# Turning the queries a unit sooner, one semaphore per cache gather, and a projection split over two units, in a two-layer attention and mixture kernel

## What is computed

```python
# attention (query and key are normed and rotated first, k and v go into the cache)
k_all, v_all = k_blocks[block_tables], v_blocks[block_tables]      # window of 256 keys + own 64
scores = einsum('bghtd,bgsd->bghts', qg, k_all) * SCALE
p = softmax(where(allowed, scores, -inf))
o = einsum('bghts,bgsd->bghtd', p, v_all)
y = einsum('bto,do->btd', o, Wo)
# experts
logits = clip(y @ gate_w.T, -50, 50)
top_w, top_idx = top_k(logits, 2); rw = softmax(top_w)
deltas = softmax(expert_atom_weights) @ atoms
weighted = deltas * sigmoid(importance)                            # sparse change of W per expert
out = y @ W.T + segment_sum(y[:, cols] * (rw . weighted[top_idx]), rows)
x = x + out
```

## Time and profile before

| | |
|---|---|
| median of 3 runs | 985.54 us (982.99 to 990.58) |
| the profiled execution | 991.06 us, its span 989.5 us |
| busy: TensorE matmul, VectorE, ScalarE, GpSimd | 90%, 66%, 39%, 44% |
| chain of work that ended last | PE 50%, DVE 16%, DMA 14%, issue 8% |
| stages | layer 0 to 455, attention to 807, lists to 827, expert tiles to 989.5 |
| granted clock of TensorE, mean | 0.94 to 455; 0.73 in 455 to 500; 0.87 in 500 to 525; 0.92 to 1.00 in each pair from 525 to 782 |

### The profile page before, as it was taken

One profiled execution on the slowest core, in us unless ns is written; L12 is line 12 of the kernel. 1 busy time (PEld: TensorE's weight loads), 2 busy tenths in 40 slices (PEclk: granted clock), 3 DMA queues, 4 the chain that ended last, 5 costly groups with the idle time before them and its releaser, 6 DMA issues.

```text
span 989.5 us, 15012 instructions
## 1 busy us (share of the span) xinstructions
PE 888.9 (90%) x4085; PEld 637.7 (64%) x4085; DVE 651.2 (66%) x1875; ACT 382.9 (39%) x869; POOL 431.0 (44%) x492
## 2 busy tenths in 40 slices
PE   5699998999899999967898999998999985999994
PEld 5688656874687478525566666665656654888773
DVE  5654589867886799495657767777766762444332
ACT  2522232224222332464545556766655530111110
POOL 3302334444344300005434665556565523666773
PEclk8599998999999999995879999999999996999998
DMA  8645454023302310544223344434333204743772
GB/s 230 239 127 197 159 198 138 1 49 81 92 1 46 120 43 1 173 147 118 77 60 93 76 115 104 113 104 128 102 97 90 61 23 130 223 148 87 126 114 31
DMA packets 66360, 105.44 MB, mean 107 GB/s; under 512 B 29811, under 2 KB 31107, under 8 KB 66158
## 3 DMA queue, kind: packets, MB, share of 16 engines
q0 software_dynamic: 30368, 50.69, 20.2%
q1 hardware_dynamic: 34974, 52.14, 17.0%
q10 hardware_dynamic: 944, 1.74, 0.6%
HBM read 91.63 MB, written 37.49 MB: 130 GB/s over the span
## 4 chain that ended last, share of the span: by engine, by line
PE 50%; DVE 16%; DMA 14%; issue 8%; POOL 4%; ACT 4%; SPq 2%; DVEq 0%; POOLq 0%; ACTq 0%
PE bank L799 14%; PE bank L810 8%; PE bank L948 6%; PE bank L933 6%; DMA mine<-list_dram 6%; PE bank L922 4%; PE bank L913 3%; PE bank L832 3%; DMA q_t<-q_dram 3%; POOL out_dram L2044 2%; DMA up_raw<-in_up_t 2%; DMA out_dram<-z_sb,mine 2%; PE bank L892 2%; PE bank L942 2%; DVE raw L1612 2%
## 5 line engine op out<-in xcount | busy, mean ns | idle before, releaser
L549 POOL DMA_INDIRECT kv_t<-kv_dram,own_new x64 | 68.9, 1076 | 179.3 <-DMA kv_dram<-kv_out 111.6
L933 PE MATMUL bank<-pT,kv_t 128*128 128x256 f32 (+1 forms) x384 | 115.6, 422 | 0.0
L832 PE MATMUL bank<-wqkv,x1T 128*128 128x512 f32 x256 | 112.1, 593 | 1.4 <-ACT x1T L1098 1.4
L1680 DVE CUSTOM_DVE_ANT_0 prob<-bank,mask 128x320 f32<-128x320 f32 x128 | 57.8, 487 | 71.8 <-PE bank L913 65.4
L1187 ACT ACTIVATE pT<-bank 128x384 f32<-128x384 f32 x128 | 55.8, 486 | 118.9 <-PE bank L922 118.3
L534 POOL DMA_INDIRECT kv_t<-in_kv_cache,own_cache x64 | 67.0, 1047 | 57.8 <-PE bank L933 39.3
L1086 ACT ACTIVATE silu<-bank,gs 128x512 f32<-128x512 f32 x44 | 30.2, 690 | 158.2 <-PE bank L799 158.2
L832 PEld LDWEIGHTS bank<-wqkv,x1T 128*128 128x128 f32 x256 | 47.7, 190 | 57.5 <-issue 57.5
L933 PEld LDWEIGHTS bank<-pT,kv_t 128*128 128x128 f32 (+1 forms) x384 | 64.1, 193 | 30.1 <-issue 22.2
L799 PE MATMUL bank<-hT_hi,gate_w 128*128 128x512 f32 x176 | 72.7, 413 | 6.9 <-DVE hdn L1523 5.3
L1256 ACT ACTIVATE zT_hi<-bank 128x512 fp32r<-128x512 f32 x44 | 26.3, 598 | 131.9 <-PE bank L1024 131.9
(11 more groups left out here) (313 smaller groups left out, 2005.2 us busy)
## 6 DMA issues: line engine op xcount, KB each, us to landing
table_dram<-wexp POOLq DMA_DIRECT2D x16, 512.0 KB, 2.9
xr<-in_x SPq DMA_DIRECT2D x4, 1024.0 KB, 6.8
yx_dram<-x SPq DMA_DIRECT2D x16, 256.0 KB, 2.3
q_dram<-q_out SPq DMA_DIRECT2D x16, 256.0 KB, 2.1
kv_dram<-kv_out SPq DMA_DIRECT2D x16, 256.0 KB, 2.3
early_stage<-table_dram SPq DMA_DIRECT2D x8, 512.0 KB, 8.1
q_t<-q_dram SPq DMA_DIRECT2D x16, 256.0 KB, 3.6
stage<-table_dram SPq DMA_DIRECT2D x16, 256.0 KB, 3.2
```

What stands on the lines that cost most here:

```text
L549: pool.indirect_dma_start(kv_t[q % KVB][0:rows, c, :], None, kv_dram, bass.IndirectOffsetOnAxis(own_new[0:rows, at:at + 1], 0), bounds_che ...
L832: mm = pe.matmul(bk(2 * (j % 2) + half), x1T[:, k, j * P:(j + 1) * P], wqkv[:, k, half * T:(half + 1) * T], start=(k == 0), stop=(k == KT ...
L933: mm = pe.matmul(bk(O_BANKS[q % 2])[:, gp * 2 * P:(gp + 1) * 2 * P], kv_t[q % KVB][0:rows, c, v:v + 2 * HD], pT[0:rows, n % 2, c, :, :].re ...
L1680: dve.tensor_tensor_reduce(prob[s % PROBS][:, :], bk(s % 2)[:, 0:KEYS], mask[:, s // 4 % 2, :], MASKED, MASKED, ALU.add, ALU.min, mx[:, s ...
```

## The change

1. SyncE issues `load_q(p + 2)` and `store_y(p - 2)` (instead of `store_y(p - 1)`) after the pair's first `load_piece`.
2. TensorE turns the next pair's queries at the end of the unit with at 0, after `values`, instead of in the unit with at 1. ScalarE's `qT_copy` now waits for the last score that reads the old `qT_hi`, VectorE's stands before the two `normalize`. `y_copy(p - 2)` stands in ScalarE's unit with at 0, after `kT_copy`, instead of `y_copy(p - 1)` at 3.
3. `project_o` is made in two halves of two k-steps, one at the end of the unit with at 2, one at the end of that with at 3. `y_ps` is given after the second.
4. The cache gathers of chunk 0 and of chunk 1 have a semaphore each (`cache_in`), and each gather of new rows waits for the cache gather of its chunk alone. `round_entry` goes; VectorE converts the entry's row number (one step more in `place_entry`).
5. The tail: `project_o(14)` comes after `logits(15)`, `project_o(15)` after `places(15)`; the last pair's `oT` has a buffer of its own; the sums of the counts are made inside `places(15)`; the steps to the row numbers are fewer and stand first (`rows_ready`), those to the experts' numbers come after; loading `mine` waits for the first list's entries alone, and for the second's from tile 22 on. Constants for this are made before the loop.

```diff
@@ gather_cache, gather_new
-                                        bounds_check=POOL_ROWS - 1, oob_is_err=False).then_inc(kv_gathered[q % KVB], 16)
+                                        bounds_check=POOL_ROWS - 1, oob_is_err=False).then_inc(cache_in[c], 16)
...
                 at = q * NCH + c
+                pool.wait_ge(cache_in[c], 16 * max(q + 1, 2))
+                pool.sem_inc(taken, 1)
                 pool.indirect_dma_start(kv_t[q % KVB][0:rows, c, :], None, kv_dram,
@@ SyncE
-                    if p >= 1:
-                        store_y(p - 1)
-                    if p + 2 < PAIRS:
-                        sp.wait_ge(qT_ps, p + 2)
-                        load_q(p + 2)
+                        if at == 0 and p >= 2:
+                            store_y(p - 2)
+                        if at == 0 and p + 2 < PAIRS:
+                            sp.wait_ge(qT_ps, p + 2)
+                            load_q(p + 2)
+                store_y(PAIRS - 2)
                 store_y(PAIRS - 1)
 
-                sp.wait_ge(entry_stored, 32 * PAIRS)
-                sp.wait_ge(tiles_ready, 1)
+                sp.wait_ge(rows_ready, 1)
+                sp.wait_ge(entry_stored[0], 16 * PAIRS)
                 for i in range(ALL_TILES):
+                    if i == TILES:
+                        sp.wait_ge(entry_stored[1], 16 * PAIRS)
@@ TensorE
+                    if p == PAIRS - 1:
+                        for n, part in enumerate((ab, counts)):
+                            mm = pe.matmul(bk(5)[:, 4 * E:6 * E], ones_sq[:, :], part[:, :, :].rearrange("p a e -> p (a e)"),
+                                           start=(n == 0), stop=(n == 1))
...
                     if n + 2 < UNITS:
                         score(n + 2)
-                    if at == 1 and p + 1 < PAIRS:
-                        if p >= 2:
-                            pe.wait_ge(y_ready, p - 1)
-                        turn_q(p + 1)
...
                     if n >= 1:
                         values(n - 1)
+                    if at == 0 and p + 1 < PAIRS:
+                        if p >= 2:
+                            pe.wait_ge(y_ready, p - 1)
+                        turn_q(p + 1)
...
                         if p + 1 < PAIRS:
                             pe.wait_ge(qT_ready, 2 * p + 4)
-                        project_o(p - 1)
+                            project_o(p - 1, range(KT // 2))
+                    if at == 3 and 1 <= p < PAIRS - 1:
+                        project_o(p - 1, range(KT // 2, KT))
 
                 final = PAIRS - 1
                 values(UNITS - 1)
                 places(final - 1)
                 logits(final)
+                project_o(final - 1)
+                places(final)
+                pe.wait_ge(y_ready, final)
                 project_o(final)
-                places(final)
-                pe.wait_ge(entry_ready, PAIRS)
-                pe.matmul(bk(5)[:, 4 * E:6 * E], ones_sq[:, :], counts[:, :, :].rearrange("p a e -> p (a e)"),
-                          start=True, stop=True).then_inc(all_ps, 1)
@@ ScalarE
                     act.wait_ge(qT_ps, p + 1)
+                    if p >= 1:
+                        act.wait_ge(score_ps, 4 * p)
...
-                    if q >= 2:
+                    if 2 <= q < B - 2:
                         act.wait_ge(y_ps, q // 2)
+                    to = oT if q < B - 2 else oT_last
+                    if q == B - 2:
+                        act.wait_ge(experts_ready, LATE)
...
                     if at == 0 and p >= 2:
+                        y_copy(p - 2)
                         route_exp(p - 2)
                     if at == 3:
                         oT_copy(2 * p)
-                        if p >= 1:
-                            y_copy(p - 1)
...
                 route_exp(final)
+                y_copy(final - 1)
                 y_copy(final)
@@ VectorE
-                    dve.tensor_reduce(entry_row[:, p, :], chosen[:, :, :], AX, ALU.add).then_inc(entry_ready, 1)
+                    step(dve.tensor_reduce(entry_row[:, p, :], chosen[:, :, :], AX, ALU.add))
+                    dve.tensor_copy(entry_at[:, p, :], entry_row[:, p, :]).then_inc(entry_ready, 1)
...
+                    if at == 1 and p + 1 < PAIRS:
+                        qT_copy(p + 1)
                     if n + 1 < UNITS:
                         normalize(2 * n + 2)
                         normalize(2 * n + 3)
-                    if at == 1 and p + 1 < PAIRS:
-                        qT_copy(p + 1)
@@ GpSimd
-                    pool.wait_ge(kv_gathered[q % KVB], q // KVB * GATHERS + 16 * 3)
-                    pool.sem_inc(taken, 1)
                     gather_new(pool, q)
```

More of the change, by code:

```diff
@@ L524, in bass_adaln_ffn_kernel @@
         taken = sem("taken")
+        cache_in = [sem(f"cache_in{c}") for c in range(2)]
         kv_gathered = [sem(f"kv_gathered{u}") for u in range(KVB)]
@@ L563, in bass_adaln_ffn_kernel @@
         l1_consts = sem("l1_consts")
[L564 removed]
+        L1_CONSTS = 16
         kT_ps = sem("kT_ps")
@@ L588, in bass_adaln_ffn_kernel @@
         entry_ready = sem("entry_ready")
-        entry_rounded = sem("entry_rounded")
-        entry_stored = sem("entry_stored")
+        entry_stored = [sem(f"entry_stored{a}") for a in range(2)]
         mask_ready = sem("mask_ready")
@@ L940, in logits, with project_o @@
                     pe.wait_ge(oT_ready, 2 * p + 2)
+                    rows = oT if p < PAIRS - 1 else oT_last
                     for k in range(KT):
-                        mm = pe.matmul(bk(5)[:, 0:E], oT[:, k, :, :].rearrange("p b t -> p (b t)"), wr[:, k, :], start=(k == 0), stop=(k == KT - 1))
+                        mm = pe.matmul(bk(5)[:, 0:E], rows[:, k, :, :].rearrange("p b t -> p (b t)"), wr[:, k, :], start=(k == 0), stop=(k == KT - 1))
                     mm.then_inc(lg_ps, 1)
-                def project_o(p):
-                    for k in range(KT):
-                        mm = pe.matmul(bk(6), oT[:, k, :, :].rearrange("p b t -> p (b t)"), wo[:, k, :], start=(k == 0), stop=(k == KT - 1))
-                    mm.then_inc(y_ps, 1)
+                def project_o(p, part=range(KT)):
+                    rows = oT if p < PAIRS - 1 else oT_last
+                    for k in part:
+                        mm = pe.matmul(bk(6), rows[:, k, :, :].rearrange("p b t -> p (b t)"), wo[:, k, :], start=(k == 0), stop=(k == KT - 1))
+                    if KT - 1 in part:
+                        mm.then_inc(y_ps, 1)
                 def places(p):
@@ L1853, in _ @@
-                tstep(dve.tensor_reduce(packs[:, :], packing[:, :, :], AX, ALU.add),
-                      dve.scalar_tensor_tensor(out=at_row[:, :, :], in0=tile_0[:, :, :], scalar=float(P), in1=at_row[:, :, :],
-                                               op0=ALU.mult, op1=ALU.add))
-                tstep(dve.tensor_copy(packs_i[:, :], packs[:, :]),
-                      dve.tensor_copy(at_row_i[:, :, :], at_row[:, :, :]))
-                dve.sem_inc(tiles_ready, 1)
+                tstep(dve.tensor_tensor(passed[:, :, :, :], ends[:, :, :, :], row_step[:, :, :].unsqueeze(2).to_broadcast(by_tile), ALU.mult))
@@ L1860, in low_rows @@
+                tstep(dve.tensor_reduce(packs[:, :], packing[:, :, :], AX, ALU.add))
+                dve.tensor_copy(packs_i[:, :], packs[:, :]).then_inc(tiles_ready, 1)
                 def low_rows(i):
```

98 lines of the change are left out of this document (49 added, 49 removed).

## The result

The changed kernel takes 996.99 us as a median of 20 runs (990.78 to 1005.62), the kernel before 986.20 beside it (979.19 to 996.00). The ratio is 1.0113, 95% interval 1.0086 to 1.0140: slower by 11 us, where I had forecast 12.7 less. The profiled execution took 997.24 us with a span of 995.6; before it was 991.06 and 989.5.

A forecast was written before the change was run, and what follows sets the result against it. In the attention loop PE is nine tenths busy; idle came from a gather stall with half clock behind it and VectorE's chain. -0.2 (start) - 10.0 + 1.7 - 4.2 = -12.7 us, giving 973 us, range 965 to 985.

The forecast's parts named there:

- The gather stall and the clock behind it: At 487 us PE's 3.36 us stall falls to 0.3 to 0.7; -10.0 if the clock stays full, -2.7 if it falls.
- S0: Start of the first score in a pair's first unit; S2 and S3 are those of its third and fourth units.
- The two waits of PE as one: In each pair, waits for `q_t` and before the third unit's score total 1.54 us, ended by VectorE's 7.90 us chain.
- ScalarE's wait behind `y_ps`: In u3, the fourth unit, `oT_copy` waits for the projection's second half, so it starts about 0.11 us after S0.
- `y_sb` meeting `turn_q`: In a pair's first unit, `y_copy` ends near S0 + 3.7 and `turn_q` waits 0.3 us, which PE can spare.
- The tail: After the last pair, reordered projections and fewer steps bring the first fetch sooner: -4.2 us, ends -3 and -5.
- the store that I had next in line: In the tail, the store of `project_o(15)`'s rows lands at 817.3 us, next in line and level with `mine` at 817.9.
- +1.7: Attention loop: +3.2 us for ScalarE's slip in 11 pairs, less 1.5 for late `q_t`; bounds -3 and +9.
- S2 to S3 becomes about 6.7, S3 to S0 5.1; the sum is the same.: Half a projection, 1.84 us, moves from a pair's third unit to its fourth at no cost in PE time.
- The slip of ScalarE: From S0 to S2, late `kT_hi` delays VectorE 0.43 us; +0.29 a pair for 11 pairs, 0 in the last pairs.
- the -0.14 that I named as a bound: Lower end of the split's cost per pair: up to 0.14 us won if ScalarE overlaps better than counted.
- Rival 4: In the loop the clock halves once every pair, 1.4 us each, +19, early clock gain lost too: 999 us; chance 0.09.

The follow-up runs named there:

- the split alone: Kernel before with only the projection cut in two halves, in u2 and u3 (third and fourth units of a pair); 1006.99 us, ratio 1.0195.
- the queries alone: Kernel before with only the next queries turned, loaded and copied a unit sooner and `y_copy` moved to ScalarE's first unit; 980.31 us, ratio 0.9918.
- the gathers alone: Kernel before with only a semaphore per cache gather, and two freed semaphores gone; 980.20 us, ratio 0.9894.
- the projection whole: Changed kernel with `project_o` undivided again at the end of the unit with at 2; queries, gathers and tail as changed; 975.54 us.
- the two-buffer kernel: Changed kernel with two buffers for `oT` and one instead of two for `y_sb`, the split kept; 971.39 us.
- the kernel with the old loop: Changed kernel with the attention loop of the kernel before on all engines, only gathers and tail changed; 985.12 us.
- the longer VectorE: The two-buffer kernel plus one superfluous mask of 0.46 us on VectorE in the first unit of each pair; 999.55 us.

## Why the prediction was wrong

Right were these steps. The gather stall and the clock behind it: -10.0 predicted, -9.9 in the profile, -9.4 in the medians of that part alone. That the two profiles agree with the sum so closely is in part luck: the split alone and the queries alone still have the stall, and get from the first score to S0 of the third pair in 47.6 and 48.6 us, where the kernel before took 52.0 and the gathers alone 42.5. The two waits of PE as one, ended by VectorE's 7.90 us and not by the queries: with the queries sooner the clean pair is the same to 0.02 us. The mechanism of ScalarE's wait behind `y_ps`, its place, its order, and `y_sb` meeting `turn_q`, were foreseen. The tail: -4.2 predicted, -3.3 found; PE waits 0.59 us for `ab` of the last pair before `places(15)`, so the first tile step came 2.5 sooner and not 3.4, and the store that I had next in line wasn't it: `mine` was.

Wrong were three steps, all in the loop, where I had +1.7 and the spans show +19.6: a cost put at nothing, a wait sized too small, and a clock left out.

1. **"S2 to S3 becomes about 6.7, S3 to S0 5.1; the sum is the same."** It isn't: 6.79 + 5.47 = 12.26 for 8.52 + 3.29 = 11.81. The halves take 1.89 and 1.91 from their start to the next group (612.34 - 610.45, 617.80 - 615.89), where I divided 3.68 by two, though the whole one takes 3.61 to its next group. And `values` takes 1.69 from its start to the second half behind it (614.20 to 615.89), where the score behind it started after 1.43 (573.21 to 574.64). +0.45 a pair, 5.9 us, costed at 0 with no bound above. The second part could have been read before: in the kernel before, `values` takes 1.69 too where `places` and not a score stands behind it:

```profile
564.69 1.76 PE L933 MATMUL bank<-pT,kv_t 128*128 128x256 f32 x6
566.38 0.40 PE L954 MATMUL bank<-ab,tri 128*128 128x16 f32 x2
```

Why a score can start sooner behind `values` than another group does I haven't tested.

2. **The slip of ScalarE, "+0.29".** It is 0.51. VectorE waited 0.62, not 0.43: `kT_hi` starts 2.94 after S0 where I had 2.73 (the exponentials and copies take 1.98, not 1.83, and start at 0.96), and VectorE has it at 3.42, not 3.17. The late pairs have it too (S0 to S2 is 8.77 and 9.21 there, beside 8.25 and 8.52 with the projection whole), where I had 0. 6.6 us where I had 3.2. By the two-buffer kernel the wait is worth 0.71, of which 0.2 is what the split gives VectorE; the -0.14 that I named as a bound was a real gain, hidden beneath the loss. The Trainium skill's statement that ScalarE's queue is strictly first in, first out (PSUM — Partial Sum Buffer, Engine vs sequencer instructions) holds here: the exponentials waited 3.21 us behind a copy that they don't need.
3. **The clock, which I left out of the forecast.** I argued that the clock stays at full in most pairs with waits of 1.5, and read from one profile of before (10 us at the lower level in 505 to 790) that it would stay so. But at 1.5 us it doesn't. In the kernels with the queries moved, waits of 0.49, 0.80, 1.09, 1.13, 1.25, 1.26, 1.46 and 1.70 go with 0, 3, 3, 7, 17, 14, 31 and 44 us at the lower level in one profile each, and with 86, 87, 90, 92, 109, 101, 122 and 126 us in the mean of the whole runs (the kernel with 1.25 still has the stall of the gathers in its 109). Rival 4 had this mechanism with a chance of 0.09, one fall a pair at 1.4 us; seven stretches came, 30.7 us in all, and 3.4 us of it cost 1.5. What it had wrong is that the early gain would be lost with it. The wait itself isn't longer than before (1.46 for 1.54), and whole runs don't show more time at the lower level than before: by the mean clock of its runs the kernel before had 128 us of it, the changed one 122. My sum had counted on 7.3 us of time from the clock at 490 (-10.0 against -2.7); 6 us at 0.37 are 2. So what the gathers won there came back in the loop, as in the kernel with the old loop.

In the spans the account of the loop closes: 13 x 0.96 = 12.5 of work, (30.7 - 10.2) x 0.47 = 9.6 of clock (the price of a us is worked out at the longer VectorE above), less some 2 for the late `q_t` of before, are 20.1 for 19.6. In the medians it is poorer: 12.5, less 2.9 of the stall, 3.3 of the tail, 2 of `q_t` and 6 x 0.37 = 2.2 of clock, and 0.7 of the expert tiles more, are near +3, of 11 measured. Some 8 us I can't place. They don't seem to lie in the split: the whole projection takes 21.4 away, of which 20.4 are placed, and the split alone adds 17.4, of which work places all. What doesn't add up are the other parts. Alone the gathers give 9.4 and the queries 9.1, and the tail 3.3 in the spans, 21.8 together; in one kernel, with the projection whole, they give 13.6 (989.14 to 975.54). Both single gains are mostly clock. No run here tells why they don't add.

Open stays why the split alone, with two waits a pair of 0.69 and up to 1.61, costs no more clock than before, and why the kernels with the old loop and 1.54 to 1.57 us show anything from 10 to 41 us in one profile each. The wait's length isn't the only thing that decides; that lengthening it costs clock, and shortening it gives clock back, is shown by the pair of kernels with two buffers that differ in VectorE's work alone: the clocks of their runs, 0.951 to 0.956 and 0.934 to 0.941, don't overlap.

## What to carry to other kernels

That the halves of a step add up to the whole doesn't make dividing it free. What waits for the end of the step waits longer, and so does all that stands behind the waiting instruction in its engine's queue: look there first. A gap that the division opens pays only with work put into it, in the same change. And where TensorE has a wait in every round of a loop, price it by what the clock does behind it too: here an operation of 0.46 us cost 2.1 a round.

## What the runs showed of the hardware

A single wait of 3.36 us was followed by 17 us at the lower level in the kernel before, the same stall in two other kernels (3.33 and 2.92 us) by 3.4 and 6.8 us. Recurring waits of 1.1 to 1.7 us, 20 to 27 us apart, were followed in some of the pairs by stretches of 3.4, 10.2 or 13.7 us, in the kernels with the queries moved by and large the more the longer the wait, and waits of 0.49 by none. In a loop where PE is busy nine tenths a us at the lower level cost 0.45 to 0.47 us in the profiles, and went with 0.37 us over whole runs. The Trainium skill (TensorE: Matmul & The Clock Gate, A second HAM failure mode: psum-queue depth-cycling) says of a kernel that cycles its PSUM queue that short idles of PE between its groups, if frequent enough, make the clock go back and forth between half and full. The traces agree in what is seen, with 3 to 44 us at half clock in the loop; the cause of the idles is another here, VectorE's chain. That rule, not the one on a wait for a transfer that the prediction leant on, is the nearer one for this loop.

Runs of one kernel on one chip differ by up to 3.4% (980.02 to 1013.55 us), and their times go with the time at the lower level. One profile is one draw: the kernel before had 10 us in the loop in its profile, its gathers-alone sibling with nearly the same waits 20.
